# Moving the layer-norm statistics of a later block ahead of key transpose, scores and top-2 routing at a block boundary

## The reference

```python
q = phi(xn @ W_Q.T); k = phi(xn @ W_K.T); v = xn @ W_V.T     # 8 heads of 64, phi = elu + 1
# over time t, per head, gamma = sigmoid(decay_log):
S = gamma * S + outer(k_t, v_t);  z = gamma * z + k_t
y_t = (S.T @ q_t) / (z . q_t + 1e-6)
attention = (y * sigmoid(xn @ W_g_w.T + W_g_b)) @ W_O.T
# ffn: dense layer plus a top-2 of 8 routed low-rank (4) part
w, idx = top_k(softmax(xn @ gate_w.T), 2)
ffn = xn @ W_lin.T + b_lin + sum_k w_k * (xn @ left[idx_k]) @ right[idx_k]
```

## Time and profile before

| | us |
|---|---|
| median of 2 runs | 460.68 (460.14 to 461.22) |
| the profiled execution | 460.79 |
| span of its slowest core, 2 | 459.7 |
| TensorE matmul busy, same core | 321.5 (70%) |
| VectorE busy | 205.3 (45%) |
| ScalarE busy | 130.7 (28%) |
| GpSimd busy | 32.2 (7%) |
| chain that ended last | PE 56%, ACT 13%, DVE 13%, issue 9%, POOL 4% |

### The profile page before, as it was taken

One profiled execution on the slowest core, in us unless ns is written; L12 is line 12 of the kernel. 1 busy time (PEld: TensorE's weight loads), 2 busy tenths in 40 slices (PEclk: granted clock), 3 DMA queues, 4 the chain that ended last, 5 costly groups with the idle time before them and its releaser, 6 DMA issues.

```text
span 459.7 us, 6493 instructions; the slowest of 8 cores (456.2 to 459.7 us)
## 1 busy us (share of the span) xinstructions
PE 321.5 (70%) x2031; PEld 145.3 (32%) x2066; DVE 205.3 (45%) x807; ACT 130.7 (28%) x281; POOL 32.2 (7%) x96
## 2 busy tenths in 40 slices
PE   0005975228889988448989986468989896689866
PEld 0003331102444434213334433223344344233431
DVE  5040534032564446344555347143565266445641
ACT  3643221744123233224304142321110241220000
POOL 8200002100000000300000000400000001200000
PEclk9999977557999999559889998668999996599987
DMA  7999990000320330000221010000111100001111
GB/s 175 190 276 164 161 160 8 1 0 1 93 75 18 93 91 1 1 1 1 91 93 46 3 47 0 2 0 0 47 48 46 47 0 3 0 6 43 46 47 46
DMA packets 12851, 24.96 MB, mean 54 GB/s; under 512 B 2929, under 2 KB 7153, under 8 KB 12818
## 3 DMA queue, kind: packets, MB, share of 16 engines
q0 software_dynamic: 7856, 7.49, 11.6%
q1 hardware_dynamic: 4962, 17.05, 11.2%
HBM read 23.63 MB, written 8.39 MB: 70 GB/s over the span
## 4 chain that ended last, share of the span: by engine, by line
PE 56%; ACT 13%; DVE 13%; issue 9%; POOL 4%; DVEq 1%; DMA 1%; another core or an unknown queue 0%; ACTq 0%; SPq 0%; POOLq 0%
PE pQK L790 13%; PE pG L587 8%; PE pQK L799 7%; PE pA L396 5%; PE pQK L396 4%; PE pO L583 4%; PE pV L583 3%; ACT scr1b L285 2%; DVE S_sb L721 2%; PE pQK L794 2%; PE pT L339 2%; PE pQK L805 2%; ACT gsig L595 2%; ACT scr1b L288 2%; DVE A_sb L632 1%
## 5 line engine op out<-in xcount | busy, mean ns | idle before, releaser
L587 PE MATMUL pG<-wg_sb,xnfm 128*128 128x512 bf16 x128 | 57.7, 451 | 31.7 <-DVE den_r L733 26.8
L790 PE MATMUL pQK<-wlin_sb,xnfm 128*128 128x512 bf16 x248 | 64.4, 403 | 0.4 <-issue 0.2
L813 DVE TENSOR_TENSOR out_sb<-pQK,x_sb 128x512 f32<-128x512 f32 x32 | 22.1, 692 | 79.5 <-PE pQK L805 79.5
L595 ACT ACTIVATE gsig<-pG 128x512 bf16<-128x512 f32 x16 | 9.6, 597 | 115.6 <-PE pG L592 104.6
L799 PE MATMUL pQK<-wo_sb,ygfm 128*128 128x512 bf16 x124 | 32.5, 383 | 0.6 <-issue 0.6
L790 PEld LDWEIGHTS pQK<-wlin_sb,xnfm 128*128 128x128 bf16 x256 | 24.1, 102 | 27.7 <-issue 5.9
L583 PE MATMUL pO<-wv_sb,xnfm 128*128 128x512 bf16 x56 | 26.9, 481 | 4.5 <-DVE den_r L733 4.5
L411 ACT ACTIVATE phir<-phiw 128x512 bf16<-128x512 f32 x32 | 19.8, 628 | 35.9 <-DVE phiw L405 35.9
L583 PE MATMUL pV<-wv_sb,xnfm 128*128 128x512 bf16 x56 | 23.3, 416 | 6.7 <-DVE den_r L733 6.7
L632 DVE TENSOR_TENSOR A_sb<-pA,masks 128x128 bf16<-128x128 f32 x64 | 18.0, 282 | 22.1 <-PE pG L619 22.1
L484 POOL TENSOR_SCALAR ind<-e,cols 128x8 f32<-128x8 f32 x16 | 4.6, 304 | 322.2 <-DVE dmpB L472 322.2
(11 more groups left out here) (139 smaller groups left out, 490.6 us busy)
## 6 DMA issues: line engine op xcount, KB each, us to landing
x_sb<-x SPq DMA_DIRECT2D x16, 512.0 KB, 8.7
out<-out_sb SPq DMA_DIRECT2D x16, 512.0 KB, 2.9
wlin_sb<-wlin POOLq DMA_DIRECT2D x1, 2048.0 KB, 58.8
wq_sb<-wq POOLq DMA_DIRECT2D x1, 1024.0 KB, 22.7
wk_sb<-wk POOLq DMA_DIRECT2D x1, 1024.0 KB, 35.3
wv_sb<-wv POOLq DMA_DIRECT2D x1, 1024.0 KB, 41.4
wg_sb<-wg POOLq DMA_DIRECT2D x1, 1024.0 KB, 47.1
wo_sb<-wo POOLq DMA_DIRECT2D x1, 1024.0 KB, 60.9
```

Source lines behind the costliest of these rows:

```text
L587: TE.matmul(pG[:, :], xnfm[:, 1024 * k + cs * 128 : 1024 * k + cs * 128 + 128], wg_sb[:, FH * k : FH * k + FH], start=(k == 0), stop=False)
L595: s_gs = s_sca.inc(SE.activation(gsig[:, (c % 2) * FH : (c % 2) * FH + FH], pG[:, :], AF.Sigmoid))
L790: TE.matmul(pQK[bank][:, :], xnfm[:, 1024 * k + cs * 128 : 1024 * k + cs * 128 + 128], wlin_sb[:, D * k + 512 * n : D * k + 512 * n + 512] ...
L813: ins = VE.tensor_tensor(out_sb[:, cp * D + 512 * n : cp * D + 512 * n + 512], pQK[bank][:, :], x_sb[:, cx * D + 512 * n : cx * D + 512 * ...
```

## The change

In the branch for the last chunk of a block, A_stats(c+8) and A_pre2 are called before ktp_stage(c+1), E_sc(c+1) and C_top2 instead of behind them. No function is changed, and no other place in the order.

```diff
@@ -879,13 +879,13 @@
                 A_ln_tp(c + 4, bank2=True)
                 B_proj((c + 1) // 4)
                 C_log_mm((c + 1) // 4)
-                ktp_stage(c + 1)
-                E_sc(c + 1)
-                C_top2((c + 1) // 4)
                 if c + 8 < NCHUNK:
                     A_stats(c + 8)
                 if (c + 1) // 4 + 1 < NBLK:
                     A_pre2((c + 1) // 4 + 1)
+                ktp_stage(c + 1)
+                E_sc(c + 1)
+                C_top2((c + 1) // 4)
```

## The result

The changed kernel takes 451.35 us (median of 11 runs, 450.69 to 454.09), the kernel before 461.04 (10 runs). In some executions the cores of one die are slowed together; three such (467.80 and 471.88 us of the run with only A_stats moved, 475.84 of the kernel before) are left out of all medians and ratios here.

What follows compares the result with a forecast made beforehand. At two block boundaries VectorE's wait for the statistics before S_sb was taken to delay TensorE's gate matmul. Chain 2.0 and two clock terms of 0.6: 460.79 - 2.0 - 0.6 - 0.6 = 457.6 us, range 453.5 to 461.5.

Steps and rivals of the forecast that it cites:

- (1) to (5): Statistics chain, delayed masks and routing, then wtu to gate matmul: gate matmul 1.0 us sooner per changed boundary, 2.0 together.
- (6): TensorE's clock at the changed boundaries: gate matmul to bias matmul and first output matmuls, a gain of 0.6 us each.
- second term: First eight output matmuls: one clock fall in three expected, 1.1 us against 1.67 now, a gain of 0.6.
- rival B: Boundaries as the third, and one of the two clock falls following boundary one gone: 453.6 us, chance 0.15.
- lower bound of 455.3: Earliest span end by the bounds of (6), with both changed boundaries as the third: 460.79 - 5.5.
- Rival A: Clock rises at the same moment regardless, so gate matmuls begun 1.0 us earlier save only 0.5: 459.8 us, chance 0.23.
- Rival C: Longer TensorE idling between scores and state matmuls, chunks 4 to 11, brings two more clock falls: 463.2 us, chance 0.16.
- D: Table loads before Ln and again before Exp in the statistics chain, 2.56 us per boundary: 462.7 us, chance 0.04.

Runs made afterwards that it cites:

- split run: Only A_stats moved ahead of key transpose, scores and routing, against the kernel before, with A_pre2 left behind them: 451.1 us.
- late A_pre2 with spare matmuls: 8 spare TensorE matmuls in C_rest at boundaries one to three, added to the kernel with A_stats early and A_pre2 behind the next chunk's C_rest: 445.27 us.
- shorter chain: The kernel before, with the four GpSimd operations in A_pre2 of blocks 2 and 3 replaced by one VectorE operation: 457.65 us.
- the pad: The kernel before, with a VectorE write of 1200 bf16 columns (1.06 us) behind A_pre2 at both changed boundaries: 457.25 us.
- A_stats early, A_pre2 late: A_stats ahead of key transpose, scores and routing, A_pre2 behind F_scan and C_rest of the next chunk, shown against the changed kernel: 444.25 us.

## Why the prediction was wrong, point by point

(1) to (5), the chain, held. The chain ahead of ktm is 5.08 us long for 5.0. It starts 0.61 us after e for a forecast 0.74. The first mask comes 4.5 us later after e than before (6.03 against 1.57). S_sb is 0.31 behind wtu and the gate matmul 4.87 behind it, on the nose, with wt last, not den_r. e to gate was forecast at 18.2 and is 18.1; the two boundaries gave 2.2 us for 2.0. The split run supports it: with A_pre2 left behind, 4.0 us per boundary were expected and 4.2 and 4.1 came.

(6), the clock, is the step that failed. It was sized at 1.2 us (0.6 and 0.6) and measured 5.8: 1.7 us from gate to first output and 4.1 us in the blocks behind. (The 0.8 us in the code ahead of boundary one and behind boundary three are not counted.) Its second term was the first output group of boundary two, and that went as a whole (block two, 1.8 of the 4.1). What the sum left out is the two falls in block one, 70 us in which the change touches nothing: it put them at no change, without a reason, and only rival B took one of them. The runs show that they go: with the change no core has both, seven of eight have neither, and a block stretch without them is 3.4 us shorter. So the lower bound of 455.3, meant as the best that the rows allow, was no bound. Without them it is 455.3 - 2 x 1.67 = 452.0; the measured 451.35 is still 0.7 below, about the size of the 0.8 us that are not counted.

Rival B, the large one, came nearest with 453.6 and had 0.15. Its mechanism, falls of block one that go, is right and its size short, since it let one of two go. It also had both boundaries like the third, and that holds for the mean only: at boundary one gate to output is 7.1 on four cores and 8.4 to 8.8 on four, with 7.6 at boundary three. Rival A (the clock swallows half the gain) is refuted. Rival C expected falls to be added, and more went. One of the falls that it named did come: the first output group of boundary one is slow on three cores, where before it was on none. That falls can be added at all is shown by the late A_pre2 with spare matmuls, one in each block on every core; that C's longer pause adds them is not shown. The table load of D isn't there: from the first pass at 180.81 to ktm at 185.89 takes 5.08 us, as long as without one, and the timeline holds no load. The Trainium skill's ScalarE: Activation LUTs, section on table sets, agrees in that one set holds exp and ln.

The rule of the Trainium skill, TensorE: Matmul & The Clock Gate, part 1, that activity releases the clock, I had weighed against the change, because a pause is added ahead of F_scan. The trace agrees with the rule and not with my use of it: a pause that counts is the one ahead of the gate stretch. Before, TensorE idled 3.68 us ahead of L548 and then 6.06 more with only four transposes in between; the change leaves the 3.68 and cuts the 6.06 to 0.56.

```profile
194.77 0.58 PE L548 MATMUL pT<-ident_s,wt 128*32 128x128 bf16 x4 [3.68 <-ACT wt L528]
```

Filling the 6.06 us with spare matmuls, with nothing else changed, gave 9.8 us.

What stays open: why a given start of the gate stretch leaves two, one or no falls in the block behind, and so by which of its two effects, the sooner start or the shorter pause, the change removed those of block one. The runs show that it isn't the start alone (shorter chain against the change: 0.1 us apart in e to gate, 6 us apart in time), nor the order alone, and that neither more nor less delay is better in itself. They also show that the falls of a block begin, but for one of 136, at three places, each behind small matmuls and a wait. I can say from a trace where a fall may come and what it costs, and can't forecast whether it comes.

## What to carry to other kernels

Where the clock of TensorE rises and falls within a kernel, a reordering has two effects of different kinds: the wait on the path, which can be worked out to a tenth of a microsecond from rows, and the number of clock falls in the repeated stretches behind, which comes in steps (1.7 us each here) and can be more than twice as large. Count the falls in every stretch before and after, and widen the range by all of them, not only by those next to the change. A gain of 2% here can be had by the change, by spare matmuls in a pause, and in part by an added delay; only the version that also returns the wait itself (A_stats early, A_pre2 late) adds its gain on top.

## What the runs showed of the hardware that I hadn't expected

A longer wait made the kernel faster: 1.06 us more VectorE work on the path at each of two boundaries took 3.8 us off the time. And the cores settle into one pattern: seven of eight cores before had block stretches of 73.6 and 72.0, and all eight with the pad have 70.3 and 70.3, though they reach boundary one at times 3.0 us (before) and 4.5 us (pad) apart. The length of a block stretch was the number of its falls and nothing else: 70.3, 71.6 to 72.1, or 73.6 us in 192 stretches of 12 kernels.
